# One table with a place for every piece, in place of the time tables that units share, in a two-layer transformer kernel on one core

## What is computed

```python
# layer 0: adaLN block, 16 heads of 16, rotary halves
ada = silu(cond) @ ada_w.T + ada_b            # gates, scales and shifts of both norms
h = layernorm(x) * (1 + s1) + sh1
q, k, v = split(h @ qkv_w.T + qkv_b);  q, k = rope(q), rope(k)
x = x + (softmax(q @ k.T / 4) @ v @ proj_w.T + proj_b) * g1
h2 = layernorm(x) * (1 + s2) + sh2
x = x + (gelu(h2 @ fc1_w.T + fc1_b) @ fc2_w.T + fc2_b) * g2
# layer 1: RMS norms, conditions from a small gated net, rotary pairs
tp = swiglu(cond @ w_t1 + b_t1) @ w_t2 + b_t2
h = rmsnorm(x, g1) * (1 + scale1) + shift1
x = x + attention(h, w_qkv, w_ao)             # same shape, 16 heads of 16
h = rmsnorm(x, g2) * (1 + scale2) + shift2
x = x + swiglu(h @ w_fc + b_fc) @ w_fo + b_fo
```

## Time and profile before

| what | us |
|---|---|
| median of three runs | 792.26 (790.42 to 793.54) |
| span of the profiled execution | 789.7 |
| TensorE busy in it | 748.3 (95%) |
| VectorE busy | 626.9 (79%) |
| ScalarE busy | 477.6 (60%) |
| GpSimd busy | 291.4 (37%) |

### The profile page before, as it was taken

One profiled execution on the slowest core, in us unless ns is written; L12 is line 12 of the kernel. 1 busy time (PEld: TensorE's weight loads), 2 busy tenths in 40 slices (PEclk: granted clock), 3 DMA queues, 4 the chain that ended last, 5 costly groups with the idle time before them and its releaser, 6 DMA issues.

```text
span 789.7 us, 13682 instructions
## 1 busy us (share of the span) xinstructions
PE 748.3 (95%) x4800; PEld 465.6 (59%) x4800; DVE 626.9 (79%) x1097; ACT 477.6 (60%) x761; POOL 291.4 (37%) x267
## 2 busy tenths in 40 slices
PE   5989889999999999999999999999999999999697
PEld 4543334475546754566546654668547685677497
DVE  3988998888779987898888899878878879755354
ACT  2127774787467765778568867665556646566232
POOL 1502204443544435452464444322344132423243
PEclk9979999999999999999999999999999999999899
DMA  8548340231131411232121333241031412000000
GB/s 322 148 140 257 87 148 25 83 95 42 41 95 28 108 42 42 67 90 59 37 73 42 95 108 97 66 108 42 27 94 28 109 41 64 6 1 1 28 1 27
DMA packets 31603, 59.45 MB, mean 75 GB/s; under 512 B 6064, under 2 KB 10800, under 8 KB 31280
## 3 DMA queue, kind: packets, MB, share of 16 engines
q1 hardware_dynamic: 31536, 58.58, 25.5%
HBM read 39.42 MB, written 18.87 MB: 74 GB/s over the span
## 4 chain that ended last, share of the span: by engine, by line
PE 74%; DVE 7%; issue 4%; POOL 3%; ACT 3%; DMA 2%; SPq 2%; ACTq 0%; DVEq 0%; POOLq 0%
PE ring L1039 19%; PE ps_o L969 12%; PE ps_b L1056 12%; PE ring L939 9%; PE ring L954 8%; PE ring L903 5%; DVE top L1235 4%; PE ring L1009 3%; PE ring L916 2%; ACT pr L1491 2%; PE ring L980 2%; SPq L847 1%; POOL sines L1605 1%; PE ring L885 1%; DMA qt<-top_t 1%
## 5 line engine op out<-in xcount | busy, mean ns | idle before, releaser
L1235 DVE TENSOR_REDUCE top<-ring 128x2 f32<-128x1024 f32 x256 | 307.3, 1220 | 47.1 <-PE ring L954 44.6
L1491 ACT ACTIVATE pr<-ring 128x1024 f32<-128x1024 f32 x256 | 255.7, 1023 | 80.7 <-PE ring L939 74.1
L1648 POOL TENSOR_TENSOR act_l<-mlp,act_h 128x256 fp32r<-128x256 f32 x128 | 102.9, 804 | 237.4 <-DVE act_h L1317 237.4
L969 PE MATMUL ps_o<-pr,va 128*17 128x512 f32 x1024 | 132.2, 597 | 0.1
L939 PE MATMUL ring<-qt,kt 49*128 49x512 f32 x512 | 113.4, 462 | 6.7 <-DMA qt<-top_t 2.8
L954 PE MATMUL ring<-kt,qt 48*128 48x512 f32 x512 | 112.4, 456 | 7.3 <-DVE top L1235 3.8
L1528 ACT ACTIVATE mlp<-ring,col 128x256 f32<-128x256 f32 x128 | 60.4, 472 | 84.4 <-PE ring L1039 71.5
L939 PEld LDWEIGHTS ring<-qt,kt 49*128 49x128 f32 x512 | 46.4, 184 | 86.3 <-issue 40.3
L1039 PE MATMUL ring<-hh,wl 128*128 128x256 f32 x384 | 84.1, 301 | 2.8 <-DVE hh L1292 1.2
L1303 DVE SCALAR_TENSOR_TENSOR mlp<-mlp 128x256 f32<-128x256 f32 x128 | 58.4, 457 | 35.4 <-ACT mlp L1535 25.0
L954 PEld LDWEIGHTS ring<-kt,qt 48*128 48x128 f32 x512 | 48.1, 187 | 60.2 <-issue 19.4
(11 more groups left out here) (89 smaller groups left out, 1022.9 us busy)
## 6 DMA issues: line engine op xcount, KB each, us to landing
scratch<-high SPq DMA_DIRECT2D x16, 512.0 KB, 3.8
scratch<-low SPq DMA_DIRECT2D x16, 512.0 KB, 4.2
qt<-scratch SPq DMA_DIRECT2D x64, 128.0 KB, 2.6
kt<-scratch SPq DMA_DIRECT2D x64, 128.0 KB, 2.7
mlp<-in_w_split SPq DMA_DIRECT2D x20, 256.0 KB, 3.0
qt<-scratch SPq DMA_DIRECT2D x64, 64.0 KB, 2.6
kt<-scratch SPq DMA_DIRECT2D x64, 64.0 KB, 2.7
xs<-in_x SPq DMA_DIRECT2D x4, 512.0 KB, 4.6
```

Source lines behind the costliest of these rows:

```text
L969: last = nc.tensor.matmul(ps_o[32 * h:32 * h + HD + 1, :], va[:, u % 2, t, QUAD * g + h, :], pr[:, slot, :], start=(t == 0), stop=(t == T ...
L1235: nc.vector.tensor_reduce(top[:, n % 2, 0:4 * T].rearrange("p (e c) -> p e c", e=2)[:, :, c], pair[:, :, :], AX_X, ALU.max, negate=True).t ...
L1491: nc.scalar.activation(pr[:, at % NP:at % NP + 2, :], pair[:, :, :], ACT.Exp, scale=SCALE).then_inc(free, 1)
L1648: nc.gpsimd.tensor_tensor(act_l[:, at % 2, :], src, act_h[:, at % 2, :].bitcast(F32), ALU.subtract).then_inc(act_l_in, 1)
```

## The change

All tables of ticks go. One table, `ORDER`, holds for each pair of engine and kind of piece the numbers of its places in the program, 0 to 2239, one for each piece, and `program()` sorts by them. The 2240 pieces are the same, and so is every line from `PROGRAM = program()` down: what an engine does in a piece, what it waits for, how banks are dealt out. Places are compared only within the list of one engine, and through `scores` and `peaks` between engines. All 32 quads and 8 units may now differ from each other.

```diff
-FIRST_AT = (-1491,
- -1023,
...
-QUAD_KIND = (0, 1, 1, 1, 2, 3, 3, 4)
-POST_KIND = (0, 0, 0, 1, 2, 2, 2, 3)
-PRE_KIND = (0, 0, 1, 1, 2, 2, 2, 2)
...
-LOAD_AT = {'row': -1007,
- 'trig': -1230,
...
+ORDER = {
+        ("act", "silu"): (0,),
...
+        ("pe", "net_1"): (10,),
...
+        ("sp", "load"): (63, 2, 21, 3, 50, 11, 1, 39, 291, 187, 203, 480),
...
 def program():

-    return [p[1:] for p in sorted(ticked(), key=lambda p: p[0])]
+    at = {kind: iter(places) for kind, places in ORDER.items()}
+    return [piece for _, piece in sorted((next(at[piece[:2]]), piece) for piece in all_pieces())]
```

More of the change, by code:

```diff
@@ L200, in top_pieces @@
-def top_pieces(n):
-    return [("pe", "top", n), ("act", "top", n), ("sp", "top", n)]
-def quad_pieces(n):
-    at = QUAD_AT[QUAD_KIND[n // NQ]][n % NQ]
-    more = n + 1 < NALL
-    pieces = []
-    for m in range(T * QUAD // 2):
-        pieces.append((at["scores"][m], None, "scores", n, m))
-    for m in range(T * QUAD // 2):
-        pieces.append((at["peaks"][m], None, "peaks", n, m))
-    pieces += [(tick, *piece) for tick, piece in zip(at["top"], top_pieces(n))]
-    pieces += [(at["values"][t], "pe", "values", n, t) for t in range(T)]
-    if n + 2 < NALL:
-        pieces += [(at["fill"], "sp", "fill", n + 2)]
-    return pieces + [(tick, engine, "output", n) for tick, engine in zip(at["output"], ("act", "pe", "dve"))]
@@ L430, with quad_pieces @@
+    pieces += [("pe", "net_2", part) for part in range(NET_PARTS)] + [("dve", "net_2")]
+    return pieces + [("sp", "load", name) for name in LOADS]
+LOADS = ("row", "trig", "ada1", "ada2", "grow", "t1", "t2", "x1", "wf0", "wf1", "x2", "x3")
 LAST = NU - 1
 TURNED = ("h1", "h2", "h2_rest")
+def quad_pieces(n):
+    pieces = [(None, "scores", n, m) for m in range(T * QUAD // 2)]
+    pieces += [(None, "peaks", n, m) for m in range(T * QUAD // 2)]
+    pieces += [("pe", "top", n), ("act", "top", n), ("sp", "top", n)]
+    pieces += [("pe", "values", n, t) for t in range(T)]
+    if n + 2 < NALL:
+        pieces += [("sp", "fill", n + 2)]
+    return pieces + [("act", "output", n), ("pe", "output", n), ("dve", "output", n)]
@@ L455, in post_pieces @@
         if u < LAST:
-            pieces.append((at["proj"][2 * half + 1], "pool", "residual", u, "proj", half))
-    pieces += norm_pieces(u, 1, at["norm"])
+            pieces.append(("pool", "residual", u, "proj", half))
+    pieces += norm_pieces(u, 1)
     if u == LAST:
-        pieces += norm_pieces(u, 2, at["norm2"])
-        pieces += [(at["bias"][2 * i + half], "pool", "bias", u, name, half) for i, name in enumerate(("proj", "fc2"))
-                   for half in range(2)]
-    for n, ticks in enumerate([at["split"]] + ([at["split2"]] if u == LAST else [])):
+        pieces += norm_pieces(u, 2)
+        pieces += [("pool", "bias", u, name, half) for name in ("proj", "fc2") for half in range(2)]
@@ L470, in post_pieces @@
         for f in range(KF):
-            up, down = at["up"][half * KF + f], at["down"][half * KF + f]
-            pieces += [(up, "pe", "up", u, half, f)]
-            pieces += [(up + d, engine, name, u, half, f) for d, (engine, name) in zip(at["after_up"], follow)]
-            pieces += [(down, "pe", "down", u, half, f)]
-        pieces.append((down + at["after_down"][0], "dve", "residual", u, "fc2", half))
+            pieces += [("pe", "up", u, half, f)] + [(engine, name, u, half, f) for engine, name in follow]
@@ L476, in post_pieces @@
+            pieces += [("pe", "down", u, half, f)]
+        pieces.append(("dve", "residual", u, "fc2", half))
         if u < LAST:
-            pieces.append((down + at["after_down"][1], "pool", "residual", u, "fc2", half))
+            pieces.append(("pool", "residual", u, "fc2", half))
     return pieces
 def pre_pieces(u):
-    at = PRE_AT[PRE_KIND[u]]
-    pieces = norm_pieces(u, 0, at["norm"])
+    pieces = norm_pieces(u, 0)
     for c in range(NC):
-        pieces += [(at["qk"][c], "pe", "qk", u, c), (at["take"][c], "act", "take", u, c)]
+        pieces += [("pe", "qk", u, c), ("act", "take", u, c)]
```

392 lines of the change are left out of this document (91 added, 301 removed), and 82 rows, old and new, of the table ORDER.

## The result

| what | before | after |
|---|---|---|
| median of runs, us | 792.9 (790.42 to 797.11, 4 runs) | 825.28 (820.95 to 826.73, 4 runs) |
| ratio | | 1.039 (95%: 1.035 to 1.043) |
| span of the profiled execution | 789.7 | 819.1 (its time: 820.95) |
| VectorE busy, same 1097 instructions | 626.9 | 657.6 |
| start of the first `peaks` of quad 0, of quad 6 | 40.7, 131.7 | 55.9, 146.8 |

The page of the kernel after, to be read beside the earlier trace rows: span, busy times, the clock, and the shares of the chain of waits.

What follows compares the result with a forecast made beforehand. VectorE was taken to bound 40.7 to 110.8 us, TensorE 131.7 to 730, with waiting chains at both ends. Terms 3.5 - 4.6 - 3.0 - 3.0 - 1.8 = -8.9 us gave 783.4 us, range 772 to 796.

Steps and rivals of the forecast that it cites:

- Bounds: -6, and +5: Limits in us on the gain of 3.0 us from less TensorE idle time between 131.7 and 730 us.
- The start, +3.5: Before the first `peaks`: late `t1` delays `net_1` and `qk`, 3.5 us lost; bounds 0 and +7, the latter with clock still low.
- Behind that point the chain is the same: After the eight `qk` matmuls, ending 3.3 us late, the steps to the first `peaks` were taken as unchanged.
- 2 us more to do: TensorE's added work before the first `peaks`, a turn and the rest of `net_2`, about covered by 2.7 idle us.
- Chunk 3 was costed at nothing: Weight chunk 3 ahead of the first fill waits for chunk 0's split; the spill was to hide it, costing nothing.
- VectorE in the first quads, -4.6: Quads 0 to 5: splits and norm statistics leave, 7.1 us off VectorE, 2.5 charged later, 4.6 won; bounds 7.1 and 0.
- Transitions and idle time, -6.0 together: 131.7 to 730 us: 30 fewer changes between matmul tile kinds, -3.0 us, and less TensorE idle time, -3.0 us.
- The end, -1.8: Last `output` and following turn: `down` matmuls fill both gaps, 1.4 us, and earlier norm rows give 0.4; bounds -3 and +1.
- The slower one: Rival: start costs +7 us at `net_1`, quads return nothing, later terms -1.5 and -1; 796.8 us, chance 0.18.
- Its two signs: Slower rival decided by first `peaks` at 47.7 us or later together with quad 5 starting no earlier than 115.
- The test named for the forecast: Forecast wrong if the middle stretch, some 592 us forecast in place of 598, is no shorter, whatever the ends do.
- two thirds of the gain: Share of the forecast gain that the prediction claimed for the middle stretch and quads 0 to 5.

Runs made afterwards that it cites:

- e13: Kernel before with `t2` loaded first and `t1` fourth, nothing else moved: 793.0 us against 792.9, first `peaks` at 41.4.
- e12: Kernel after with `t1` loaded first again and weight chunk 3 behind the first two spills and first fill: 820.1 us, first `peaks` at 51.2.

## Why the prediction was wrong, step by step

- **What it failed at.** "What an engine does in a piece" was taken to last as long at any place. Each term moved VectorE's and GpSimd's pieces at the mean duration of the earlier trace rows, and none asked what GpSimd does at that moment. The price of that wait wasn't in any bound or rival. The trace of before had it in single places: a row of L1184 of 1.3 us against a mean of 0.38, and two widening copies of 2.51 us beside a `sine` at 30.3 us. "Bounds: -6, and +5" for idle time in the middle held new waits only as a count of moved pieces; it measured +13.8 (25.5 - 11.7), with some 10 us at the lower clock on top, which no term of the middle had.
- **The start, +3.5, measured +15.2** at the first `peaks`. The load's reading was right: `net_1` at 16.40, forecast 16.5.

```profile
16.40 3.58 PE L924 MATMUL ring<-small,xs 128*128 128x4 f32 x16 [3.99 <-DMA xs<-in_w_t]
19.84 7.25 PE L745 MATMUL ring<-hf,wf 128*128 128x512 f32 x12
...
43.39 6.97 PE L939 MATMUL ring<-small,wf 128*128 128x4 f32 x32
50.22 5.70 PE L912 MATMUL ring<-xs,add 128*128 128x512 f32 x8
55.85 0.51 PE L796 MATMUL ring<-kt,qt 48*128 48x512 f32 x2
```

  The clock had not risen, the bound of +7 covered that. "Behind that point the chain is the same" was the wrong sentence: VectorE's four rows took 3.41 and four widening copies 4.95 us beside `sine` and `low`, and TensorE waited 2.09 us more.

```profile
27.37 3.41 DVE L1023 TENSOR_SCALAR xn<-xs,mv,rstd 128x256 f32<-128x256 f32 x4
...
33.23 4.95 DVE L1254 COPY add<-small 128x128 f32<-128x128 f32 x4
```

  The "2 us more to do" was right as a sum of work: before too does all of `gates` and six of the eight parts of `net_2` ahead of its first `peaks`. But there they lie in the chain's waits, and here 12.7 us of them stand behind that wait, at the lower clock. `e13` shows that the load costs nothing alone. Chunk 3 was costed at nothing: the first fill was issued at 41.22, 0.4 us behind it, but with both loads moved (`e12`) the `peaks` came no earlier than with one.
- **VectorE in the first quads, -4.6, measured -0.1** (90.9 for 91.0 us, quads 0 to 5). The parts: 2.9 us gained where 7.1 were taken off VectorE, 2.7 given back in the next quad where 2.5 were charged. VectorE is busy 0.85 of the stretch, not over 0.9: the maxima's waits for TensorE's `peaks` grew from 5.4 to 8.0 us. The bound of 0 held.
- **Transitions and idle time, -6.0 together.** With the hold, +15.4. With GpSimd's hold away the middle is 7.0 us shorter. That the sum fits is luck: TensorE's busy time falls by 7.6 us where 3.0 were forecast, its idle time rises by 0.6 where it was to fall by 3.0. Either the transitions were too small, or what was taken for idle was waiting with an instruction open; the runs don't tell these apart.
- **The end, -1.8, measured -0.4** from the start of the last row of `values` to the first `up` of unit 7 (16.50 for 16.87 us), and -1.0 from the last `output` to the last `down` (50.6 for 51.6). Over all, from the first `peaks` of quad 30 to the last `down`, 2.0 us are gained, but mostly not at the gaps that were named. These were filled as forecast, and the chain behind them took the gain: the second half's turn waits 2.84 us. The first row is before's.

```profile
745.29 1.11 PE L885 MATMUL ring<-eye,xn 128*128 128x128 f32 x4 [0.16 <-DVE xn L1184]
```

```profile
764.25 0.63 PE L822 MATMUL ring<-eye,ot 128*128 128x128 f32 x4
...
773.75 0.66 PE L727 MATMUL ring<-eye,xn 128*128 128x128 f32 x4 [2.43 <-DVE xn L1026]
777.25 1.12 PE L727 MATMUL ring<-eye,xn 128*128 128x128 f32 x4 [2.84 <-DVE xn L1026]
778.02 0.78 PE L881 MATMUL ring<-hh,wl 128*128 128x256 f32 x2
```

- **The rivals.** The slower one had the right place for a part (`net_1`) and the wrong size, and expected the middle to gain. Its two signs came (first `peaks` at 55.9, quad 5 at 123.0), but nothing in it has a hold between VectorE and GpSimd. The test named for the forecast, "wrong if the middle stretch is no shorter", was met. The sentence behind it has a slip: two thirds of the gain is the middle alone (6.0 of 8.9); with quads 0 to 5 it is 10.6 us, more than the whole.

## What to carry to other kernels

Before VectorE's work is moved in a list, look at what GpSimd does beside its new place: here a short instruction from SBUF to SBUF paid the rest of GpSimd's instruction, and the next one paid the next. A mean duration from a kernel whose order avoids this is no price for an order that doesn't. When an order gains and loses at once, take the suspected partner out of both kernels: the distance between them, +14.9 with GpSimd's work and -10.6 without, says more than either time. Then give the partner its time back in short instructions, since taking it out also takes away the wait for its results.
